# Four stacked graph layers on one core: the expert layer's start, its combining and its batch norm arranged anew

## The reference

```python
h = feats * rsqrt(deg_out)[:, None]
m = segment_sum(h[src], dst) * rsqrt(deg_in)[:, None]
x = m @ W_gc + b_gc + (feats @ W_res + b_res)
vals, idx = top_k(x @ Wg + bg, 2)            # 64 experts, two picks per node
gates = softmax(vals)
# expert e: gelu(rows @ w1[e] + b1[e]) @ w2[e] + b2[e], 256 -> 512 -> 256
y = x + sum over k of gates[:, k] * expert[idx[:, k]](x)
mean = mean(y, axis=0); var = mean((y - mean) ** 2, axis=0)
y = (y - mean) * rsqrt(var + 1e-5) * gamma + beta
out = layernorm(feats + y)                    # over the 256 features
```

## Time and profile before

| | us |
|---|---|
| median of 3 runs | 2098.84 |
| lowest, highest | 2097.65, 2101.59 |
| the profiled execution, its own time | 2101.84 |
| its span, first to last instruction | 2099.6 |
| TensorE busy in the span | 1814.2 (86%) |
| VectorE busy | 908.4 (43%) |
| ScalarE busy | 498.6 (24%) |
| GpSimd busy | 464.1 (22%) |
| mean granted TensorE clock | 0.941 of full speed |
| HBM traffic | 545 MB, 259 GB/s over the span |

### The profile page before, as it was taken

How to read it: one execution, slowest core, us unless ns; L and a number is a source line. 1 busy time by engine, 2 the same in 40 slices (tenths; PEclk the granted TensorE clock), 3 DMA queues, 4 the chain that set the end, 5 groups by cost and what they waited for, 6 DMA issues and landing times. The chain is left out here.

```text
span 2099.6 us, 34207 instructions
## 1 busy us (share of the span) xinstructions
PE 1814.2 (86%) x9538; PEld 1437.0 (68%) x9539; DVE 908.4 (43%) x2709; ACT 498.6 (24%) x1301; POOL 464.1 (22%) x824
## 2 busy tenths in 40 slices
PE   1988886799899999989989999989999599999811
PEld 0355555688788878867768878867777489899700
DVE  4877664444434421122221127756666222122167
ACT  0034444322223311111111111111111123322242
POOL 1022222411112100000000002216666532333203
PEclk8999998899989999999999999999999699999955
DMA  4178999999778868866658878868886599999931
GB/s 126 32 242 286 319 324 337 319 321 321 242 244 267 264 198 283 282 212 213 211 189 282 282 260 281 281 222 256 258 252 183 172 369 379 375 382 377 355 125 61
DMA packets 279196, 545.06 MB, mean 260 GB/s; under 512 B 18198, under 2 KB 201024, under 8 KB 275904
## 3 DMA queue, kind: packets, MB, share of 16 engines
q1 hardware_dynamic: 271072, 526.38, 75.9%
q0 software_dynamic: 8032, 17.60, 2.2%
HBM read 415.19 MB, written 128.72 MB: 259 GB/s over the span
## 5 line engine op out<-in xcount | busy, mean ns | idle before, releaser
L1045 PE MATMUL psum<-xsa,blk 128*128 128x512 f32 x2500 | 647.8, 408 | 18.3 <-DVEq L363 8.2
L1045 PEld LDWEIGHTS psum<-xsa,blk 128*128 128x128 f32 x2500 | 462.0, 191 | 113.3 <-issue 11.3
L1045 PE MATMUL psum<-xsb,blk 128*128 128x512 f32 (+1 forms) x1875 | 424.4, 374 | 5.9 <-DVEq L363 5.9
L1045 PEld LDWEIGHTS psum<-xsb,blk 128*128 128x128 f32 x1875 | 324.4, 192 | 69.5 <-issue 7.0
L1810 POOL TENSOR_SCALAR ve<-mv 128x1 f32<-128x1 f32 x75 | 16.9, 225 | 829.7 <-DVE mv L1521 829.7
L1406 DVE TENSOR_SCALAR onehots<-counts_scratch 128x348 bf16<-128x348 f16 x464 | 161.7, 374 | 82.3 <-issue 41.9
L947 PE MATMUL psum<-onehots 128*128 128x349 bf16 x464 | 149.4, 322 | 38.7 <-DVE onehots L1411 38.3
L950 PE MATMUL psum<-zrow 128*128 128x512 bf16 x464 | 176.4, 390 | 0.0
L524 PE MATMUL psum<-route,expert_weights 128*128 128x128 f32 x1360 | 168.3, 277 | 0.0
L524 PEld LDWEIGHTS psum<-route,expert_weights 128*128 128x128 f32 x1360 | 160.4, 194 | 0.3
L534 PE MATMUL psum<-expert_weights,route 128*128 128x256 f32 x672 | 159.1, 380 | 0.3 <-ACT route L581 0.3
(11 more groups left out here) (303 smaller groups left out, 2107.6 us busy)
## 6 DMA issues: line engine op xcount, KB each, us to landing
blk<-counts_src_on_rows SPq DMA_DIRECT2D x125, 832.0 KB
blk<-counts_src_on_rows SPq DMA_DIRECT2D x125, 768.0 KB
expert_weights<-in_L_gnn_w SPq DMA_DIRECT2D x176, 512.0 KB, 5.9
blk<-counts_dst_on_rows SPq DMA_DIRECT2D x50, 832.0 KB
counts_dst_on_rows<-band_rows SPq DMA_DIRECT2D x25, 1600.0 KB, 8.1
blk<-counts_dst_on_rows SPq DMA_DIRECT2D x50, 768.0 KB
counts_src_on_rows<-blk SPq DMA_DIRECT2D x13, 1600.0 KB, 8.6
counts_src_on_rows<-rblk SPq DMA_DIRECT2D x12, 1600.0 KB, 9.7
```

The lines of the kernel that those rows point to most:

```text
L1045: mm = e.matmul(o, blk[n][:, k * P:(k + 1) * P], XS[:, k, :, 0:Fw], start=(k == 0), stop=(k == T - 1 and not own))
```

## The change

It touches three places.

1. **Start of the expert layer.** For the last tile GpSimd scatters the rows as soon as their numbers are known, then runs `l3_pages`, then scatters the ids; for every tile the ids' two scatters come behind the rows' two, and count on a semaphore of their own, `ids_scattered`. SyncE waits for the rows' scatters alone, loads the rows of four chunks, and then waits for the page table and for the ids. `xin` moves to the end of the region `route`, where no routing scratch lies. TensorE turns the table of picks behind the first hidden product, not ahead of the first rows; VectorE copies it behind the first two chunks' rows. `pick_rows`, `pick_of` and `pick_col` move into `route`.
2. **Combining.** The barrier `experts` is gone; SyncE waits for the stored rows and for the last gelu before it loads `ybuf`. Groups are 2, 5, 6, 6 and 6 tiles. VectorE sums no tiles. Of every five tiles TensorE multiplies two by ones straight from `X4` (or from the squares), and GpSimd adds up the other three into one buffer `added`, which TensorE multiplies last.
3. **Output.** Groups are 5, 5, 5, 5, 3 and 2 tiles.

```diff
+        COMBINED = [(0, 2), (2, 7), (7, 13), (13, 19), (19, T)]
+        OUT = [(0, 5), (5, 10), (10, 15), (15, 20), (20, 23), (23, T)]
+        def group_of(t):
+            return [hi > t for _, hi in COMBINED].index(True)
+        def by_tensor(t):
+            return t % 5 < 2
...
             for c in range(RING):
                 load_w1(c, c)
                 load_w2(c, c)
+            e.wait_ge(S("rows_scattered"), 16 * TOP * T)
+            for c in range(RING):
+                load_rows(c, c)
             e.wait_ge(S("experts_known"), 1)
-            e.wait_ge(S("rows_scattered"), 2 * 16 * TOP * T)
+            e.wait_ge(S("ids_scattered"), 16 * TOP * T)
             e.dma_start(pick_rows[0:NCH, :], ...)
             for c in range(RING):
-                load_rows(c, c)
                 load_b2(c, c)
...
-            phase_end(e, "experts")
+            for n in range(RING):
+                e.wait_ge(S(f"rows_stored{n}"), 16 * turns)
+            e.wait_ge(S("gelu_made"), RING * turns + 1)
...
-            e.wait_ge(S("inputs_loaded"), 16 * (LOADS + 2))
-            e.transpose(psum[:, 6, 0:P], pick_rows[:, :], identF[:, :]).then_inc(S("ids_turned"), 1)
             turn(0, 0, 0, 0)
             turn(1, 0, 1, 1)
             hidden(0, 0, 0, 0)
+            e.wait_ge(S("inputs_loaded"), 16 * (LOADS + 2))
+            e.transpose(psum[:, 6, 0:NCH], pick_rows[0:NCH, :], identF[0:NCH, 0:NCH]).then_inc(S("ids_turned"), 1)
...
-            for n, (name, buf) in enumerate((("combined", sums_of), ("squares_added", squares_of))):
-                for g in range(T // SPLIT):
-                    e.wait_ge(S(name), g + 1)
-                    mm = e.matmul(psum[:, n, 0:F], ones[:, :], buf[:, g, :], start=(g == 0), stop=(g == T // SPLIT - 1))
-                mm.then_inc(S("bn_summed"), 1)
+            for n in range(2):
+                for t in filter(by_tensor, range(T)):
+                    e.wait_ge(S(("combined", "squared")[n]), group_of(t) + 1)
+                    e.matmul(psum[:, n, 0:F], ones[:, :], (X4[:, t, :], picked_rows[:, t, 1, :])[n], start=(t == 0), stop=False)
+                e.wait_ge(S("sums_added"), n + 1)
+                e.matmul(psum[:, n, 0:F], ones[:, :], added[:, n, :], start=False, stop=True).then_inc(S("bn_summed"), 1)
...
                 st.done(e.tensor_tensor(y0, y0, y1, ALU.add))
-                st.done(e.tensor_tensor(X4[:, b, :], X4[:, b, :], y0, ALU.add))
-                e.tensor_reduce(sums_of[:, g, :], over_tiles(X4[:, b, :]), AX.X, ALU.add).then_inc(S("combined"), 1)
+                e.tensor_tensor(X4[:, lo:hi, :], X4[:, lo:hi, :], y0, ALU.add).then_inc(S("combined"), 1)
...
-            for n in range(RING):
-                e.wait_ge(S(f"rows_stored{n}"), 16 * turns)
-            carry_wait(e)
-            phase_end(e, "experts")
+            steps = 0
+            for n in range(2):
+                for t in range(T):
+                    if by_tensor(t):
+                        continue
+                    v = (X4[:, t, :], picked_rows[:, t, 1, :])[n]
+                    e.wait_ge(S(("combined", "squared")[n]), group_of(t) + 1)
+                    carry_wait(e)
+                    if t == 2:
+                        ins = e.tensor_copy(added[:, n, :], v)
+                    else:
+                        ins = e.tensor_tensor(added[:, n, :], added[:, n, :], v, ALU.add)
+                    steps += 1
+                    ins.then_inc(S("pool_steps"), 1)
+                    e.wait_ge(S("pool_steps"), PAGE_STEPS * T + steps)
+                e.sem_inc(S("sums_added"), 1)
...
-            pipeline(e, [(2, l3_pages), (1, l3_keep), (2, l3_scatter)], unrolled=True)
+            pipeline(e, [(2, l3_first), (1, l3_keep), (2, l3_scatter), (2, l3_last), (2, l3_ids)], unrolled=True)
```

140 lines of the change are left out of this document (69 added, 71 removed).

## The result

The changed kernel takes **2079.78 us**, the median of 5 runs (2076.83 to 2085.05), against 2098.84 before. The ratio on record is 0.9892, with a 95% interval of 0.986 to 0.9924, so 1.1% faster; the two medians alone divide to 0.9909, inside that interval. The forecast was 2083.1 with a range of 2076.0 to 2091.0. The total is near it, but the gain is not where I had put it. Start and barrier hold and the squares nearly so, sums and output gave 3 us less than I had forecast, the drain that I took for gone came back in full, and some 15 us were won in code that the change does not touch.

A forecast was written before the change was run, and what follows sets the result against it. PE and the DMA engines fill the expert loop; only the stretches around it can shrink. Start -5.3, barrier -6.2, sums and squares -1.7, output -2.5 make -15.7: from 2098.84 to 2083.1 us, range 2076.0 to 2091.0.

The forecast's parts named there:

- start of the experts: Ahead of the expert loop: earlier row scatters and a later table turn start chunk 2's turn sooner, -5.3 us.
- barrier: Behind the expert loop: without the barrier, SyncE loads `ybuf` at 1993.9 and not 2000.06, -6.2 us.
- sums: Combining, first load to first centring: TensorE and GpSimd sum the tiles, 36.7 us against 39.1, -2.4.
- squares: Combining, mean to variance: GpSimd's steps nearly all follow the centrings, 20.4 us against 19.7, +0.7.
- output: Kernel's end: fewer activations behind the last tile and a smaller last store, -2.5 us.
- my two arms: Expert start: rows and ids reach TensorE separately; first hidden product ends at 1657.0, table turn at 1657.2.
- the drain moves: GpSimd's drain behind the scatters returns at combine's barrier, +4.7, 2087.8 us; chance 0.16, shared with a lost gain.
- a lost part: Barrier removal or early rows gain nothing, each losing 5 or 6: about 2089 us; 0.16 shared with the returning drain.
- The step: Combining: one GpSimd 128x256 addition with its semaphore wait takes 0.83 us, between 0.68 and 0.96.
- my second rival: Combining: VectorE waits for GpSimd as well; sums end at 37.1, not 34.9, time 2085.0 us; chance 0.25.

The follow-up runs named there:

- a_1024_ids: Changed kernel with 1024 idle bytes at the two big tables' old place, and the last tile's ids scattered ahead of the pages: 2080.51 us, one run.
- a_pad: Changed kernel with six unused tensors where the three tables of picks stood, restoring the old layout behind them: 2092.82 us, 0.9951.
- a_cols_even: Changed kernel with four idle one-column tensors where `pick_col` stood, and output in five even groups: 2095.07 us, one run.
- b_pad16: Kernel before with an idle tensor of 16 bytes per partition behind the four one-column tensors of picks: 2105.39 us, 1.0013.
- a_three_drain: Changed kernel with three tiles of five summed by TensorE and GpSimd drained once behind the expert loop: 2071.35 us, 0.9859.
- a_four_drain: Changed kernel with four tiles of five summed by TensorE and GpSimd drained once behind the expert loop: 2065.3 us, 0.9831.
- a_drain_early: Changed kernel with one more GpSimd drain, right behind the expert loop: 2075.87 us, 0.987.
- a_barrier: Changed kernel with the barrier behind the experts kept: 2078.17 us, 0.9876.

## Why the prediction was right, and where it was not

The total was right by luck. The terms that I had priced, with the drain that I had not, came to -7.8 in place of -15.7, and a gain of 15.5 that I had not priced more than filled the hole. With that gain and all my terms right the time would have been 2067.6, below my range. Point by point, forecast against runs (means over the kernels that share the piece of code):

| term | forecast | measured |
|---|---|---|
| start of the experts | -5.3 | -5.5: the turn of chunk 2 is 17.3 behind R in nine kernels, 22.8 in the four of the old order |
| barrier | -6.2 | -6.6: 7.4 for 13.9 (-6.4 in the first pair) |
| sums | -2.4 | -0.1: 38.85 in six kernels, 38.92 in four (-0.4 in the first pair) |
| squares | +0.7 | +1.3: 21.0 for 19.7 |
| output | -2.5 | -1.6: 34.7 in nine kernels, 36.3 in five (-1.3 in the first pair) |
| the drain | none (a rival, +4.7) | +4.7: 9.3 for 4.6 |
| pace of the aggregations | none | -15.5: R at 1625.1 in nine kernels, 1640.6 in five |

The measured column adds up to -23.3, beside the 22.7 of the ratio and the 19.1 of the medians. In the pair of profiled executions the start shows only as -4.4, and from R to the last expert addition it is -1.5; the means over kernels of that whole stretch are 342.8 and 349.4, -6.6. One pair would have misled me there.

- **The start** was right in size, and in mechanism where it counts, though one arm was not. I let the rows come at 1648.8, 7 us behind their last scatter; SyncE loaded them 2.4 behind it. It didn't matter, since I had the ids as the later arm. That the table is what TensorE waits for is shown by its 6.81 us of idleness there. The table itself is hardly earlier, as in my two arms: TensorE turns it 16.6 to 17.7 behind R in the nine kernels of the new order and 17.0 to 17.6 in the four of the old. What is gained is the work that used to stand behind the table and now stands ahead of it, the turns of chunks 0 and 1 and the first hidden product. For that the rows need not be as early as they are: in a_1024_ids they are first turned 11.8 behind R and not 6.7, and chunk 2 only 0.3 later than in the mean of the nine. No run keeps the old order of the scatters beside the new order on SyncE and TensorE, so what the scatters' order brings by itself is not shown.
- **The barrier** was priced rightly at its own place. The step of the prediction that failed is the sentence "Against it: by then 60 us have passed since the last scatter". Time does not pay for it: the first drain behind the scatters took 6.9 to 9.5 us in every kernel, whether it stood directly behind them or almost 70 us later. The rival "the drain moves" came true with its own price, +4.7. It deserved more than the 0.16 that it shared with a lost part, as its only contrary argument was time passed, on which no row bore.
- **The sums** gained next to nothing. The term failed in two places. The step measured 0.93 and not 0.83, still within my bounds up to 0.96. (My own sum was 0.2 short, too: 30.1 and six steps of 0.83 are 35.1, not 34.9.) And VectorE does wait for GpSimd. That is my second rival: it put the end of the sums at 37.1 behind the load, and GpSimd's last addition of them ended at 2010.95, 36.8 behind it. The rule in the Trainium skill, "SBUF — State Buffer", section "Who interferes with whom", was the better forecast: an exclusive lock on the shared port pair, held for the whole instruction by whoever issued first. The trace of the changed kernel agrees in both directions: additions end 0.57 to 0.59 behind VectorE's instruction, and VectorE's 1.76 become 2.16 to 2.20. A page's rule had the side on which my trace had no row, and I gave it 0.25 to my own 0.32.
- **The squares** lose as forecast, for the reason forecast: nearly all of GpSimd's steps stand behind the centrings. 0.6 more, for 14 steps of 0.93 where I had 0.83 (1.3), less what it did get done beside VectorE.
- **The output**: the last two activations took 1.09, as priced, but the last store was waited for 4.4 and not the 3.7 that I took (3.3 in a_pad), and the groups are worth 1.3 to 1.6 in all.
- **The aggregations** are no mis-sized term but a missing one. I had read the move of the tables as free, since it adds and removes no instruction, and counted everything ahead of the experts as equal. It was two thirds of the gain. Without it (a_pad) the change gives 10.3 of 2102.76. My sum with the moved drain would have been 11.0.

## What to carry to other kernels

- When a change frees or adds memory, compare the unchanged phases first, by the pace of one instruction group in one window. A move that adds and removes no instruction was worth 15 us here, and a few idle columns took it back.
- Ask of every wait that is removed what the waiting engine did in it. Here GpSimd's drain came back in full at the next barrier, and cost nothing once it stood where GpSimd was idle anyway.
- Work given to GpSimd beside VectorE's two-operand instructions cost both here. Look for an idle engine that waits for neither: every tile moved on to TensorE paid, up to four of five.

## What the runs showed of the hardware

- The float32 products of 128x512, at a granted clock of 1.00, came every 226.7 ns in some kernels and every 232.4 (before, a_cols_even) to 234.3 (b_pad16) in others, 2.5% and more apart, with the same instructions and the row tensors elsewhere in SBUF: fast with `xsa` at 125056 and 126080, slow at 125184, 126208, 126240 and 126272.
- GpSimd's first drain behind indirect scatters took 6.93 us in the kernel before, 7.89 in the changed one, and 9.05, 9.17, 9.22 and 9.45 directly behind the last scatter (a_three_drain, a_four_drain, a_drain_early, a_barrier); the second took 0.83.
- TensorE's granted clock in the squares was 0.66 with ten tiles of its own and 0.88 with twenty, so more work came with less time for each product.
- GpSimd's 128x256 addition took 0.72 us alone and 1.99 to 2.00 when it began inside a VectorE addition of two SBUF operands; VectorE's 128x1536 addition took 1.75 or 1.76 alone and 2.16 to 2.20 when it began inside one of GpSimd's.
- The last scatter of ids flew 8.02 us in the changed kernel and 10.20 in a_1024_ids, where it left 1.9 earlier: the table was loaded at 14.1 and 14.4 behind R.
